# Dealing the 72 projection matmuls of a half over its eight slots as 16, 8, 6, 6, 16, 8, 6, 6 in place of 9 each

## The reference

```
x = x + 0.5 * ffn(layernorm(x))     # W_base dense + bias, and 8 LoRA experts of rank 16, top 2 by softmax
x = x + attn(layernorm(x))
x = x + 0.5 * ffn(layernorm(x))

attn(x):  q = rope(x @ wq)  32 heads of 128;  k = rope(x @ wk), v = x @ wv  8 heads of 128
          scores = q k^T * 128**-0.5, allowed: j <= i and j > i - 128
          out = softmax(scores) @ v, then out @ wo
```

## Time and profile before

| | |
|---|---|
| median of 3 runs | 810.45 us (809.56 to 811.89) |
| span of the profiled execution | 807.1 us |
| what lies outside that span, by the median | 3.35 us |
| mean granted TensorE clock | 0.979 of full speed |
| one group in the loop (two halves) | 84.59 us |
| TensorE busy, DVE busy, POOL busy | 92%, 84%, 63% |

### The profile page before, as it was taken

How to read it: one execution, slowest core, us unless ns; L and a number is a source line. 1 busy time by engine, 2 the same in 40 slices (tenths; PEclk the granted TensorE clock), 3 DMA queues, 4 the chain that set the end, 5 groups by cost and what they waited for, 6 DMA issues and landing times.

```text
span 807.1 us, 14015 instructions
## 1 busy us (share of the span) xinstructions
PE 739.6 (92%) x3692; PEld 611.2 (76%) x3692; DVE 677.0 (84%) x2060; ACT 417.0 (52%) x1122; POOL 508.7 (63%) x578
## 2 busy tenths in 40 slices
PE   5989778999899989998999899999899899988998
PEld 3878557878777878787878777877788787876876
DVE  3888878988898888889888888888978898888795
ACT  2324474556655665555555555565557545654321
POOL 0384387766777667757775776577667776664720
PEclk8899999999999999999999999999999999999999
DMA  9040002100120011001100120002100210020002
GB/s 293 1 170 14 1 4 84 45 1 2 66 66 1 0 65 52 13 0 65 52 13 0 52 65 13 0 20 71 39 0 0 70 47 0 2 105 0 2 27 79
DMA packets 25986, 32.25 MB, mean 40 GB/s; under 512 B 5849, under 2 KB 14425, under 8 KB 25442
## 3 DMA queue, kind: packets, MB, share of 16 engines
q1 hardware_dynamic: 21216, 30.56, 11.5%
q10 hardware_dynamic: 4738, 1.31, 0.7%
HBM read 27.67 MB, written 4.19 MB: 39 GB/s over the span
## 4 chain that ended last, share of the span: by engine, by line
PE 51%; DVE 28%; issue 11%; ACT 5%; ACTq 2%; POOL 2%; DVEq 1%
PE bank L1106 17%; PE bank L1165 16%; DVE sm L812 4%; PE bank L1128 4%; PE bank L1149 4%; PE bank L1072 4%; DVE rot L791 3%; ACT prob L554 3%; DVE rot L782 2%; DVE wo_lo L861 2%; PE bank L1136 2%; DVE sm L805 2%; DVE prob L820 2%; DVE pT_hi_lo L826 2%; DVE oT_lo L832 2%
## 5 line engine op out<-in xcount | busy, mean ns | idle before, releaser
L377 POOL TENSOR_TENSOR pT_hi_lo<-pT_hi_lo,side 128x256 fp32r<-128x256 f32 x256 | 186.9, 751 | 118.6 <-DVE pT_hi_lo L826 118.6
L554 ACT ACTIVATE prob<-sm,nmax 128x128 f32<-128x128 f32 x256 | 101.0, 395 | 204.9 <-DVE sm L812 204.9
L370 POOL TENSOR_TENSOR swap<-swap,rope 128x512 f32<-128x512 f32 x80 | 105.8, 1322 | 95.5 <-ACT swap L528 95.5
L820 DVE TENSOR_SCALAR prob<-prob,rinv 128x128 f32<-128x128 f32 x256 | 123.9, 525 | 4.5
L528 ACT ACTIVATE swap<-bank 64x512 f32<-64x512 f32 x160 | 94.9, 593 | 11.3 <-PE bank L1106 8.7
L387 POOL TENSOR_TENSOR q_lo<-rot,q_hi 128x512 fp32r<-128x512 f32 x64 | 84.5, 1321 | 6.8 <-ACT q_hi L536 6.8
L1165 PE MATMUL bank<-wo_hi,oT_hi 128*128 128x512 f32 x256 | 79.4, 434 | 0.3 <-DVE x L839 0.3
L812 DVE TENSOR_TENSOR sm<-sm 128x128 f32<-128x128 f32 x128 | 79.3, 619 | 0.0
L1106 PE MATMUL bank<-xnT_hi,wq_hi 128*128 128x512 f32 x256 | 72.3, 395 | 6.5 <-DVE rot L782 5.3
L1106 PE MATMUL bank<-xnT_lo,wq_hi 128*128 128x512 f32 x256 | 73.4, 390 | 0.0
L1106 PE MATMUL bank<-xnT_hi,wq_lo 128*128 128x512 f32 x256 | 72.6, 396 | 0.9 <-POOL wq_lo L362 0.9
(11 more groups left out here) (148 smaller groups left out, 1705.6 us busy)
## 6 DMA issues: line engine op xcount, KB each, us to landing
raw<-in_L_attn_wq SPq DMA_DIRECT2D x32, 256.0 KB, 2.9
raw<-in_L_attn_wo SPq DMA_DIRECT2D x32, 256.0 KB, 2.7
x<-in_L_attn_x SPq DMA_DIRECT2D x4, 512.0 KB, 7.8
raw<-in_L_attn_wk SPq DMA_DIRECT2D x8, 256.0 KB, 2.5
raw<-in_L_attn_wv SPq DMA_DIRECT2D x8, 256.0 KB, 2.6
out<-x SPq DMA_DIRECT2D x8, 256.0 KB, 2.0
raw<-in_L_ffn_W_base ACTq DMA_DIRECT2D x4, 256.0 KB, 5.3
wb_keep_hi<-q_hi SPq DMA_DIRECT2D x1, 1024.0 KB, 4.8
```

The source lines that it names most:

```text
L370: nc.gpsimd.tensor_tensor(w, w, tab, ALU.mult).then_inc(t2_done, 1)
L377: last = nc.gpsimd.tensor_tensor(pT_both[:, :, blk, h, :], both.bitcast(F32), side[:, blk - 1, :].unsqueeze(1).broadcast_to([P, 2, P]), AL ...
L554: last = nc.scalar.activation(prob[:, s % 2, lo:hi], sm[:, s % 2, lo:hi], ACT.Exp, bias=nmax[:, s % 2, i:i + 1], scale=-1.0, accum_out=rsu ...
L820: last = nc.vector.tensor_scalar(prob[:, s % 2, lo:hi], prob[:, s % 2, lo:hi], rinv[:, s % 2, i:i + 1], None, ALU.mult)
```

## The change

The table of chunks changes, and with it `FIRST` and `ENDS`. In the first half of group 0 the value transposes move to behind the first twelve projections.

```diff
-CHUNKS = (9,) * SLOTS
+CHUNKS = (16, 8, 6, 6, 16, 8, 6, 6)
 FIRST = [sum(CHUNKS[:s]) for s in range(SLOTS + 1)]
 ENDS = {s: m for m in range(6) for s in range(SLOTS) if FIRST[s] < 12 * (m + 1) <= FIRST[s + 1]}
...
                         if not (last and hf == 1):
-                            project(j + 1, 1 - hf, FIRST[s], FIRST[s + 1], g + hf)
+                            if s == 0 and start:
+                                project(j + 1, 1 - hf, FIRST[s], 12, g + hf)
+                                v_transpose(j)
+                                project(j + 1, 1 - hf, 12, FIRST[s + 1], g + hf)
+                            else:
+                                project(j + 1, 1 - hf, FIRST[s], FIRST[s + 1], g + hf)
...
-                        if s == 0 and start:
-                            v_transpose(j)
```

## The result

The change makes the kernel slower: 867.59 us median of 4 runs (867.12 to 869.2) against 810.51 (809.56 to 811.89) for the kernel before on the same chip, ratio 1.0705 with a 95% interval of 1.0687 to 1.0723. I had forecast 845.5 us in a range of 815 to 862. The direction and both places were right; the loss was 57 us where the sum gave 35, and the time lies outside the range. The span of the profiled execution grew from 807.1 to 865.5 us, 58.4; what lies outside the span is 1.9 us in the changed kernel's profiled execution (867.4 less 865.5).

What follows compares the result with a forecast made beforehand. The loop was taken as two nearly equal loops, TensorE and DVE, bound by each other's waits. Even halves +1.0 and odd +3.9 us, seven times, gave 34.3; 807.1 + 35 = 842, plus 3.35 is 845.5 us, range 815 to 862.

Steps and rivals of the forecast that it cites:

- n = 60 without a wait: Even half: TensorE's 2.94 us wait for `rope_cos` of result 3 goes, since result 3 ends in slot 4.
- `p_lo` of slot 4 ahead of it late: Even half: `p_lo` starts at 34.3 us, before 31.47; slot 6's transposes wait for it, a 3.1 us stall.
- The slow clock behind it, 1.7: Behind the long stall of each half, TensorE's halved clock costs another 1.7 us.
- `x_add`: 1.1 in slot 3 of the even half, 0.4 in slot 7 of the odd one: Output projections wait for `x_add` to empty their bank: about 1.1 us in even slot 3, 0.4 in odd slot 7.
- n = 20 at 10.8, wait 5.0: Odd half: the first matmul on wq_lo starts at 10.8 us (bounds 10.0 and 11.6), stalled 5.0 by POOL's split.
- Behind n = 20, 32.5 + 1.7 + 0.4 = 34.6: Rest of the odd half: 32.5 us of TensorE work, 1.7 of slow clock, 0.4 for `x_add`.
- The base, 43.15 and 41.44: Lengths in us of one even and one odd half before the change, taken to repeat from group to group.
- Group 0's first half, 0.4: Loses 0.4 us; moving the value transposes there replaces a wait of about the same length.
- What lies outside the span, 3.35: 3.35 us outside the span, added to 842 to reach the median's scale.
- Worse than summed: Rival, chance 0.07: `x_add` holds slots 3 and 7 in both halves, about 8 us a group, 867 us.
- The even half is repaired: Rival, chance 0.18: even half gains 1.6 us, odd half loses 3.3, +1.7 a group, 823 us.
- No change: Rival, chance 0.04: DVE's own chain holds the loop, TensorE's waits only move, 810 us.

Runs made afterwards that it cites:

- even_front: Kernel before with chunks 16, 8, 6, 6, 9, 9, 9, 9 in even halves, 9 each in odd halves: 819.18 us, 1.0107.
- even_back: Kernel before with chunks 9, 9, 9, 9, 16, 8, 6, 6 in even halves, 9 each in odd halves: 823.67 us, 1.0163.
- wq_early: Changed kernel with all four pieces of wq_lo split by POOL in slot 7 of the even half: 827.29 us, 1.0213.
- even_b12: Kernel before with chunks 9, 9, 9, 9, 12, 6, 9, 9 in even halves, 9 each in odd halves: 822.91 us, 1.0148.
- wo_pool: Changed kernel with all four pieces of wo split on POOL, none on DVE: 874.49 us, 1.0781.
- x_early: Changed kernel with the first `x_add` of a pair moved from slots 3 and 7 to ahead of the minimum in slots 2 and 6: 867.85 us, 1.0738.
- before_x_early: Kernel before with the first `x_add` of a pair moved ahead of the minimum in slots 2 and 6: 830.27 us, 1.0256.
- before_wq: Kernel before with all four pieces of wq_lo split in slot 7 of the even half: 803.88 us, 0.9919.

## Why the prediction was wrong, step by step

- *n = 60 without a wait, `p_lo` of slot 4 ahead of it late.* The wait is right, and its time nearly so by luck. I had `p_lo` start 34.3 us into the half, it starts at 34.67 (405.82 - 371.15). But the 2.8 us that I moved it by were 1.6 for slot 0's late transposes and 1.2 for a `rope_cos` and a `rope_sum`. The 3.2 that it moved are 1.0 by way of slot 3's `x_add` wait, 1.6 for the 16 projections of slot 4, which I had left out, and 0.6 for `rope_sum` alone (even_front, even_back): three wrong sizes that nearly cancel. The transposes start at 35.2 and not 34.6: 0.4 of it is this start, the rest the end of `p_lo` (406.23) and 0.15 us more until the first matmul.
- *The slow clock behind it, 1.7.* Right: 1.8 in the even half, and 1.7 behind n = 20 (6.83 us from 427.11 to 433.94, 5.13 for the same work at full clock).
- *`x_add`: 1.1 in slot 3 of the even half, 0.4 in slot 7 of the odd one.* This is the term that was mis-sized. Measured as time of the stretch it is 0.96 + 0.66 in the even half and 0.85 + 1.10 in the odd: 3.6 us a group where the sum has 1.5. Slot 7 of the even half stood in the sum at nothing, without a reason. The sum's even half runs from the end of `p_lo`, so slot 3's wait is in it already; what it lacks is 0.66 there and 1.55 in the odd half, seven times about 15 us of the 23 that are missing from the span (58.4 less 35). I had followed `p_lo` and the minimum through the slots but asked for `x_add` at one place in each half.
- *n = 20 at 10.8, wait 5.0.* The matmul starts at 10.39 (427.11 - 416.72), within my bounds. The wait is 3.97, since the pieces come 0.4 sooner than I had it and TensorE is there 0.6 later: slot 0's 16 projections take 4.17 us, 417.07 to 421.24, and not 3.63. 0.3 of this is a term that I lacked. n = 12, which starts result 1, now stands in slot 0 and has to find bank 1 empty; it starts at 420.21, right behind `v_lo` (419.39 to 420.08), where TensorE could have been at 419.9.
- *Behind n = 20, 32.5 + 1.7 + 0.4 = 34.6.* It takes 36.3; the `x_add` stretches above are 1.55 of the 1.7 that is missing.
- *The base, 43.15 and 41.44.* Two of the seven even halves before are 41.6 us with the same wait (below), and the two odd halves behind them are 42.5. The changed kernel has the slow clock in all of them. Against the bases that I took this is 3.3 us more in the even halves and 1.9 less in the odd ones.
- *Group 0's first half, 0.4.* Wrong: 3.6, and 0.6 ahead of it, where its transposes now stand behind 12 projections and no longer 9. TensorE's waits in it come to 11.9 us where they were 9.1; `v_lo` alone costs 2.43 where it was 1.20. The granted clock of the half is 0.92 and was 0.96, and TensorE is busy 0.9 us longer in it. "A wait of about the same length" was argued and not priced.
- *What lies outside the span, 3.35.* I took the span of one execution and the median of three. With 1.9 us outside, as in the changed kernel, the profiled one was itself about 1.4 us faster than the median. So the span grew by 58.4 and the medians differ by 57.1.
- *The rivals.* "Worse than summed" gave 867 and that came out. Its mechanism is there, but at less than half of its weight: it had 8 us a group from `x_add` alone, and at most 3.6 of the 7.7 are `x_add`'s; wq_early shows that 4.6 to 5.6 of the odd half's are wq_lo's. That its time came out is luck. "The even half is repaired" fell with even_b12 and even_back, in which the repair by itself loses. "No change" is false as a forecast, yet its idea explains why repairs fail: in wo_pool and x_early a removed wait came back elsewhere.

The items of this list before the rivals (15 for `x_add`, seven times 0.6 for the transposes in slot 6, seven times -0.4 for the pieces that came sooner, 1.4 for the bases, 3.9 for the first half, and -0.6 behind the last, where I had 0.4 and it was -0.2) come to 21 of the 23 us. The step of the prediction that failed is thus the size of the `x_add` term, 0.4 in the odd half and nothing in slot 7 of the even one, which measured 1.95 and 0.66; behind it come group 0's first half and a slot 4 that was not followed.

What stays open: I can name each wait but not derive the length of DVE's chain in a half from first steps; what part of the `x_add` waits could be won by an order that doesn't push the minimum wasn't tried. In wo_pool and even_b12 the lost time is found where POOL works beside DVE's normalisation or `rope_sum`; no run takes POOL's work away from there without putting other work in its place, so how much of the even half's loss is this contention isn't shown.

## What to carry to other kernels

Where two engines are within a few per cent of each other, don't price a re-deal of one engine's work by the wait it removes: follow the other engine's products through every slot, and ask for each consumer (here `p_lo`, wq_lo, and the one I under-priced, `x_add`) whether it now comes late. A wait costs more than its printed idle time, here 0.25 us for a short one and 1.7 to 1.8 more where the clock falls behind it. A half that TensorE gets through sooner is no gain yet: look whether the next one is longer. Try a suspected repair in the kernel before by itself: even_b12 and before_x_early answered in one run what the sum could not.

## What I had not expected of the hardware

**The clock does not always fall behind the same wait.** Windows of before_wq, 5 us behind its wait of 2.93 and of 2.95 us for `rope_cos`, same instructions:

```profile
209.86:214.86 5.00, 5.00 (x19) 4.38 (x20) 4.92 (x16) 2.97 (x8) 3.57 (x4) 0.68 0.43 133
378.05:383.05 5.00, 5.00 (x25) 4.29 (x26) 4.92 (x16) 2.97 (x8) 3.59 (x4) 1.00 0.46 141
```

The granted clock is 0.68 once and 1.00 once, and the halves are 43.0 and 41.6 us. In the kernel before two of the seven kept the clock; in the changed kernel, whose waits there are 3.6 us and longer, none of the even halves did.

**What the kept clock gains is mostly taken back in the next half.** Windows of the kernel before, the first even half of the loop and the odd half behind it:

```profile
176.97:218.52 41.55, 38.62 (x199) 32.68 (x198) 35.48 (x106) 25.59 (x69) 27.65 (x29) 1.00 0.09 32
218.52:261.02 42.50, 40.16 (x199) 32.40 (x198) 36.91 (x113) 23.26 (x64) 31.30 (x33) 1.00 0.11 32
```

The even half is 1.6 us shorter than the 43.15 of the earlier trace rows, the odd one 1.1 longer than the 41.44, both at full clock. TensorE comes to n = 20 sooner there and waits 0.44 us for wq_lo (at 228.10). So the 1.6 us of slow clock were worth 0.5 us a group. In before_wq the odd halves behind a kept clock take 41.6 to 43.3 us and the others 40.3 to 40.4: 1.3 to 3.0 us given back for 1.5 kept.

**Beside POOL, DVE's instructions on SBUF alone are slow.** The pair of normalisations takes 0.48 us alone and 2.43 to 2.59 with POOL at work beside it, about 1.3 for each, which is the length of one piece of POOL's split (2.54 for two). `rope_sum` takes 0.68 alone and 1.77 beside POOL; `rope_cos` and `p_lo`, which read a bank, keep their 0.68 and 0.41 beside POOL's split (wo_pool, 404.35 and 404.95). So in this kernel work that is moved from DVE to POOL comes off DVE's time in full only where DVE meanwhile reads a bank: 2.4 us moved put `p_lo` 1.2 sooner. The Trainium skill (GPSIMD Engine Reference, Key points) has the two contend when a DVE instruction has two SBUF inputs or runs in a mode with two ports; `rope_sum` agrees with the first, and the normalisation, with one SBUF input, is slowed as much; no run here shows in which mode it runs.
